# Two stacked cross attentions: a block's values in one stretch, its logits among the next block's queries

## The chip, the cores and the metric

The kernel runs on one core of one Trainium2 chip. The metric is the time of one execution on the device, in microseconds (us). The kernel before took 851.07 us in the median of three runs (849.96 to 851.61).

A core has engines that run their own instruction streams and meet only at semaphores: TensorE (PE, matmuls; PEld is its load of weights), VectorE (DVE), ScalarE (ACT), GpSimd (POOL) and SyncE (SP), which here issues nearly all DMAs. TensorE writes into PSUM, eight banks of 128 partitions by 512 floats; VectorE and ScalarE empty them; GpSimd works between tiles in SBUF only.

## The reference

Two cross attentions follow one another over 2 x 2048 query rows of width 512, both against the same context of 2 x 128 rows. All is float32. The change touches the first one:

```
q = x @ Wq0 + bq0            # 4096 x 1024, 16 heads of 64
k = ctx @ Wk0 + bk0 ; v = ctx @ Wv0 + bv0      # 128 keys for each of 2 batches
attn = (q . k) * mask[None]              # mask 0/1, per batch, query and key
attn = exp(attn - max(attn)) * mask
attn = attn / (sum over keys + 1e-15)
x1   = layernorm((attn @ v) @ Wo0 + bo0 + x) * gamma + beta
```

The second attention has 16 heads of 32, no mask, a softmax and a layer norm of its own.

## The kernel before, in words

The 4096 query rows are eight blocks (NB) of 512 (QB). Products that need precision are split in three: an operand is held as a high part rounded to fp32r and a low part that is the rest, and `split_product` (L501 to L503) adds high x low, low x high and high x high into one bank.

The kernel has two passes. The first pass makes, for each block, the queries, the logits, the exponentials and the unnormalised values with their sums, and stores these in DRAM. The second pass loads them, divides, applies the output matrix and the layer norm, and runs the whole second attention. The global maximum is kept as a running maximum over the blocks, so a block's exponentials can't start before the last of its logits is masked.

The first pass of one block i, by engine:

- TensorE. `queries0(i)` makes eight chunks of 128 query columns, each of twelve matmuls, alternately into bank 1 and bank 0 (`A_BANKS`). `logits0(i, c)` makes the logits of two heads, transposed (keys on partitions, 512 queries along), three matmuls a head, into four banks in turn (`L0_BANKS`: 0, 2, 3, 4). `values0(i, j)` makes value chunks 2j and 2j+1, each four matmuls of 32 columns (L557) into bank 5 or 6 (`U_BANKS`), and then the row sums of four heads (L540) into bank 7.
- ScalarE. `x_high` (L873) rounds a block's x, `mask_float` (L881) converts the integer mask `mask_raw` to `mask_f`, `q_high` (L885) takes a query chunk out of its bank, `exponential` (L891) does four heads in place in `scores`, `save_u` (L914, L918) copies value chunks and sums out of their banks.
- VectorE. `q_low` (L1148) makes the low part of a query chunk and frees its bank. `mask_scores` (L1159) takes one head's logits out of its bank times the mask, with their maximum. `running_max` (L1165 to L1182) reduces these to one number and ends with `neg_mx`. `mask_probs` (L1189) multiplies four heads of exponentials by the mask.
- GpSimd. `x_low` (L1548) makes the low part of x for the next block, `x_and_bias` (L1556) adds a bias to the natural rows of x.
- SP. One queue of DMA issues in program order, with its waits: for i = 1 to 7 the loads of x and the mask ahead, sums of block i - 2, the stores of block i - 1's values and sums, the store and next load of the natural rows.

Every engine runs its list in order, and the lists are written out by hand. Those of the middle of the first pass are, before the change:

```
PE :  for i in 1..7:  for j in 0..3: values0(i-1, j); logits0(i, 2j); logits0(i, 2j+1)
                      queries0(i+1)
ACT:  mask_float(i); x_high(i+1); save_u(i-1); then q_high(i+1, 0..7), exponential(i, 0..3) behind 1..4
DVE:  mask_scores(i) 16 heads; running_max(i); q_low(i+1, 0..7), mask_probs(i, 0..3) behind 2..5
```

The waits that the prediction goes through are these. A value chunk c waits for its four heads to be masked (`probs_ready`) and for the save that frees its bank (`u_saved`, two chunks back). Logits of heads 2c and 2c+1 wait for the masked scores that free the bank (`masked_ready`, four heads back) and for all of the block's q_low. A query chunk waits for the q_low two chunks back; chunk 1 also waits for masked scores, since bank 0 is shared with the logits. `mask_float(i)` overwrites the mask that `mask_probs(i-1)` reads, so it waits for `probs_ready`. Behind the last block TensorE makes the second attention's keys (L489, four products into banks 1, 0, 3, 4), then `values0(7, 0..3)`, then `output_first` (L632 to L636), the first product of the second pass.

Of the kernel before, what the change touches and what calls it, by code (L numbers as in the profile page):

```python
# [28 lines left out]
def cross_attention_program(nc, x_t, x_n, mask_t, ctx_t, wq0, wk0, wv0, wo0, wq1, wk1, wv1, wo1,  # L29
# [10 lines left out]
    with ExitStack() as ctx:  # L40
# [108 lines left out]


# [6 lines left out]
        A_BANKS, L0_BANKS = [bank[1], bank[0]], [bank[0], *bank[2:5]]  # L157
        U_BANKS, SUM_BANK = bank[5:7], bank[7]

        V0_BANKS = [*U_BANKS, SUM_BANK, U_BANKS[0]]  # L160
# [98 lines left out]
        def l0_bank(i, h):  # L259

            return L0_BANKS[(h + (i == 0)) % 4]
# [221 lines left out]
        def _(pe):  # L483
# [21 lines left out]
            def queries0(i):  # L505
                pe.wait_ge(x_ready, i + 1)
                if i == 0:
                    pe.wait_ge(x_half_ready, 1)
                    pe.wait_ge(kv_done, 2)
                for c in range(C0):  # L510
# [4 lines left out]
                    if c == 1 and i > 0:  # L515

                        pe.wait_ge(masked_ready, H0 * i - (HC0 if i > 1 else 0))
                    for k in range(KC):
                        cols = slice(c * P, (c + 1) * P)
                        last = split_product(A_BANKS[c % 2][:], (wq0_hi[:, k, cols], wq0_lo[:, k, cols]),  # L520
                                             (x_hi[:, k, :], x_lo[:, k, :]), k == 0, k == KC - 1)
                    last.then_inc(q_psum_ready, 1)

            def logits0(i, c):
# [19 lines left out]
            def values0(i, j):  # L544
                b = i // NBB
                for c in range(2 * j, 2 * j + 2):
# [5 lines left out]
                    if not (i == 0 and c < 2):  # L552
                        pe.wait_ge(u_saved, (C0 + 1) * i + (c - 1 if c >= 2 else c - 2))

                    for part in range(G):
                        h, first = HC0 * c + part // 2, c * P + 32 * part
                        last = nc.tensor.matmul(U_BANKS[c % 2][32 * part:32 * part + 32, :],  # L557
# [59 lines left out]
            pe.wait_ge(q_ready, C0 * NB)  # L617
            for n in range(C1):
                if n == 1:
# [226 lines left out]
        def _(act):  # L846
# [28 lines left out]
            def mask_float(i):  # L875
# [3 lines left out]
                if i > 0:  # L879
# [894 lines left out]
```

## Time and profile before

| | |
|---|---|
| median of three runs | 851.07 us (849.96 to 851.61) |
| the profiled execution | 850.99 us, its span 849.2 us |
| granted TensorE clock, mean | 0.995 |
| TensorE, matmul busy | 829.6 us (98% of the span) |
| VectorE busy | 569.9 us (67%) |
| GpSimd busy | 448.8 us (53%) |
| ScalarE busy | 403.1 us (47%) |
| DMA, mean rate | 132 GB/s |

The span runs from the first to the last instruction of one execution; the rest of an execution's time lies around it. Busy time counts overlapping matmuls once, and a busy TensorE need not be at its peak. The first pass ends at about 359 us of the span. In a timeline, equal neighbours of one line are merged (x16 is sixteen instructions), a start is in microseconds from the start of the span, and a bracket says how long the engine was idle before the row and what ended that. The start of a matmul to the start of the next is what one costs; its own length is longer, since they overlap.

### The profile page before, as it was taken

The page shows a single profiled execution, that of the slowest core. Times are in us where ns is not written, and L with a number is a line of the kernel's source. Part 1 is how long each engine was busy: PE and PEld are TensorE (multiplying, and loading weights), DVE is VectorE, ACT ScalarE, POOL GpSimd, SP SyncE. Part 2 cuts the span into 40 slices and gives each one's busy share as a digit, 9 for nine tenths or more (in the row PEclk, how much of TensorE's full clock was granted, in tenths as well). Part 3 has the DMA queues.
Part 4 walks back from the last instruction along what each step waited for, and adds up shares of the span by engine and source line. Part 5 has one row for each costly group of instructions (what it writes and reads, how often), then busy time and mean ns, then how long its engine had stood idle before and what let it go on. Part 6 is the DMA issues. An engine that isn't in the chain of part 4 may idle for free.

```text
span 849.2 us, 12709 instructions
## 1 busy us (share of the span) xinstructions
PE 829.6 (98%) x4652; PEld 561.8 (66%) x4652; DVE 569.9 (67%) x1307; ACT 403.1 (47%) x535; POOL 448.8 (53%) x285
## 2 busy tenths in 40 slices
PE   9999999999999999898999999999999999999996
PEld 6777475665657484385667577677676775776744
DVE  3567766767667585876766766747657567667587
ACT  4416373645546454733543634444536436354262
POOL 2022403123040405235878789689687886894446
PEclk9999999999999999998999999999999999999999
DMA  9518525161625044887360531433424515311002
GB/s 309 204 46 297 191 101 214 50 223 54 251 64 200 29 186 177 226 314 191 96 170 26 167 107 51 149 99 98 151 75 112 162 37 163 100 50 51 1 26 74
DMA packets 50429, 112.37 MB, mean 132 GB/s; under 512 B 4544, under 2 KB 10944, under 8 KB 50368
## 3 DMA queue, kind: packets, MB, share of 16 engines
q1 hardware_dynamic: 49408, 111.23, 40.3%
q8 instruction: 37, 0.61, 0.3%
q10 hardware_dynamic: 960, 0.34, 0.2%
q14 instruction: 24, 0.20, 0.1%
HBM read 77.47 MB, written 34.08 MB: 131 GB/s over the span
## 4 chain that ended last, share of the span: by engine, by line
PE 68%; POOL 12%; DVE 8%; issue 5%; DMA 3%; ACT 3%; SPq 1%; DVEq 0%; POOLq 0%; ACTq 0%
PE bank L501 15%; PE bank L502 15%; PE bank L503 14%; PE bank L557 7%; PE bank L533 6%; POOL a_raw L1585 4%; POOL a_lo L1590 4%; PE bank L540 3%; POOL a_lo L1596 3%; PE bank L695 3%; DVE scores L1304 2%; DMA r_bc<-r_dram 2%; ACT a_hi L968 1%; DMA wk_sb<-wk 1%; PE bank L667 1%
## 5 line engine op out<-in xcount | busy, mean ns | idle before, releaser
L1548 POOL TENSOR_TENSOR x_lo<-x_raw,x_hi 128x2048 fp32r<-128x2048 f32 (+1 forms) x8 | 35.6, 4448 | 196.3 <-ACT x_hi L873 180.7
L501 PE MATMUL bank<-wo_lo,a_hi 128*128 128x512 f32 x320 | 127.7, 399 | 0.0
L502 PE MATMUL bank<-wo_hi,a_lo 128*128 128x512 f32 x320 | 124.8, 390 | 0.0
L503 PE MATMUL bank<-wo_hi,a_hi 128*128 128x512 f32 x320 | 124.7, 390 | 0.0
L1159 DVE CUSTOM_DVE_ANT_0 scores<-bank,mask_f 128x512 f32<-128x512 f32 x128 | 80.8, 687 | 51.9 <-PE bank L533 51.9
L1590 POOL TENSOR_TENSOR a_lo<-a_raw,a_hi 128x1024 fp32r<-128x1024 f32 x32 | 77.4, 2421 | 50.9 <-ACT a_hi L968 50.9
L501 PE MATMUL bank<-x_lo,wq_hi 128*128 128x512 f32 x256 | 101.1, 395 | 0.5 <-DVE q_lo L1148 0.5
L988 ACT ACTIVATE scores<-scores,sh 128x512 f32<-128x512 f32 x128 | 80.3, 710 | 41.0 <-DVE sh L1329 41.0
L502 PE MATMUL bank<-x_hi,wq_lo 128*128 128x512 f32 x256 | 99.7, 390 | 0.0
L503 PE MATMUL bank<-x_hi,wq_hi 128*128 128x512 f32 x256 | 99.7, 389 | 0.0
L885 ACT ACTIVATE q_hi<-bank,bq_sb 128x512 fp32r<-128x512 f32 x64 | 44.1, 690 | 100.9 <-PE bank L503 97.3
L1304 DVE TENSOR_SCALAR_CACHE_REDUCE scores<-bank 128x512 f32<-128x512 f32 x128 | 80.6, 686 | 15.2 <-PE bank L695 15.2
L1148 DVE SCALAR_TENSOR_TENSOR q_lo<-bank,bq_sb,q_hi 128x512 fp32r<-128x512 f32 x64 | 47.7, 746 | 42.3 <-ACT q_hi L885 42.2
L501 PEld LDWEIGHTS bank<-wo_lo,a_hi 128*128 128x128 f32 x320 | 60.1, 188 | 22.5 <-issue 11.0
L968 ACT ACTIVATE a_hi<-a_raw 128x1024 fp32r<-128x1024 f32 x32 | 33.9, 1060 | 85.4 <-POOL a_raw L1585 80.3
L1189 DVE TENSOR_TENSOR scores<-scores,mask_f 128x2048 f32<-128x2048 f32 x31 | 72.0, 2323 | 0.6 <-ACT scores L891 0.6
L1585 POOL TENSOR_TENSOR a_raw<-a_raw,r_bc 128x1024 f32<-128x1024 f32 x28 | 67.1, 2396 | 7.2 <-DMA r_bc<-r_dram 7.2
L503 PEld LDWEIGHTS bank<-wo_hi,a_hi 128*128 128x128 f32 x320 | 60.1, 188 | 12.9
L502 PEld LDWEIGHTS bank<-wo_hi,a_lo 128*128 128x128 f32 x320 | 60.1, 188 | 11.7
L557 PE MATMUL bank<-scores,v 128*32 128x512 f32 x512 | 61.8, 598 | 4.3 <-ACT u_out L914 2.7
L540 PE MATMUL bank<-scores,summer 128*32 128x512 f32 x512 | 65.6, 595 | 0.0
L914 ACT ACTIVATE u_out<-bank 128x512 f32<-128x512 f32 x64 | 37.3, 597 | 56.5 <-PE bank L557 55.5
(179 smaller groups left out, 1668.1 us busy)
## 6 DMA issues: line engine op xcount, KB each, us to landing
u_dram<-u_out SPq DMA_DIRECT2D x8, 2048.0 KB, 7.3
a_raw<-u_dram SPq DMA_DIRECT2D x32, 512.0 KB, 3.7
r_bc<-r_dram SPq DMA_DIRECT2D x56, 256.0 KB, 5.0
x_raw<-x_t SPq DMA_DIRECT2D x8, 1024.0 KB, 5.6
xn<-x_n SPq DMA_DIRECT2D x8, 1024.0 KB, 5.3
xb_dram<-xn SPq DMA_DIRECT2D x8, 1024.0 KB, 5.8
z<-xb_dram SPq DMA_DIRECT2D x32, 256.0 KB, 2.9
out<-z SPq DMA_DIRECT2D x6, 1024.0 KB, 7.3
```

The source lines that it names most:

```text
L501: nc.tensor.matmul(dst, lh, rl, start=first, stop=False)
L502: nc.tensor.matmul(dst, ll, rh, start=False, stop=False)
L503: return nc.tensor.matmul(dst, lh, rh, start=False, stop=last)
L533: last = nc.tensor.matmul(l0_bank(i, HC0 * c + a)[:], kk[r, c, ks], qq[r, c, :], start=(n == 0), stop=(n == 2))
L540: last = nc.tensor.matmul(dst[32 * g:32 * g + 32, :], summer[:, j, :], scores[:, G * j + g, :], start=(j == 0), stop=(j == HG - 1))
L557: last = nc.tensor.matmul(U_BANKS[c % 2][32 * part:32 * part + 32, :], v0[:, b, first:first + 32], scores[:, h, :], start=True, stop=True)
L988: nc.scalar.activation(scores[:, h, :], scores[:, h, :], ACT.Exp, bias=sh1[:, g, h:h + 1], scale=SCALE1).then_inc(probs1_ready, 1)
L1159: nc.vector.tensor_tensor_reduce(out=scores[:, h, :], in0=l0_bank(i, h)[:], in1=mask_f[:], scale=1.0, scalar=-3e38, op0=ALU.mult, op1=ALU.max,
L1189: nc.vector.tensor_tensor(four, four, mask_f[:].unsqueeze(1).to_broadcast([P, HG, QB]), ALU.mult).then_inc(probs_ready, 1)
L1304: nc.vector.tensor_scalar(scores[:, h, :], L_BANKS[h % HC1][:], 1.0, -3e38, ALU.mult, ALU.max, accum_out=mx1[:, h:h + 1]).then_inc(scores1 ...
L1585: nc.gpsimd.tensor_tensor(a_raw[:, n, :], a_raw[:, n, :], r_bc[:, n % 2, :], ALU.mult).then_inc(attn0_ready, 1)
L1590: nc.gpsimd.tensor_tensor(a_lo[:, n, :], a_raw[:, n, :], f(a_hi[:, n, :]), ALU.subtract).then_inc(a0_ready, 1)
```

## The change

The list of TensorE for blocks i = 1 to 6 is now: all four `values0(i-1, j)`; then four times two `logits0` of block i and one chunk of `queries0(i+1)`; then the other four chunks of queries. Block 7, which has no next block, keeps values and logits in turns. VectorE takes q_low of the next block's chunks 0 to 3 between each four heads of masked scores, the running maximum after that, and the four `mask_probs` behind q_low of chunks 5, 6, 7, the last two in a row. ScalarE does its four exponentials behind q_high of chunks 4 to 7; it saves two value chunks, then does x_high and the mask, then saves the others.

The values get four banks (3 to 6) in blocks 0 to 5, two (6 and 1) in block 6, four (5, 6, 2, 1) in block 7. The logits get banks 2 to 5 (block 0 as it was). Where a bank is shared a wait is added: logits 0 and 1 wait for saves 4 and 6 of the block before, value chunk 1 of block 6 for a q_low, chunk 3 of block 7 for a key product; the masked-score wait of the queries goes, but for block 1. The mask of the last block is converted in place, so its conversion doesn't wait for `mask_probs(6)`.

```diff
+        def mask_of(i):
+            return mask_f[:] if i < NB - 1 else mask_raw[:].bitcast(f32)
...
-        A_BANKS, L0_BANKS = [bank[1], bank[0]], [bank[0], *bank[2:5]]
-        U_BANKS, SUM_BANK = bank[5:7], bank[7]
+        A_BANKS, L0_BANKS = [bank[1], bank[0]], bank[2:6]
+        U_BANKS, U_AMONG, U_END, SUM_BANK = bank[3:7], [bank[6], bank[1]], [bank[5], bank[6], bank[2], bank[1]], bank[7]
+        def u_banks(i):
+            return U_BANKS if i < NB - 2 else (U_AMONG if i == NB - 2 else U_END)
...
-            def queries0(i):
+            def queries0(i, first=0, last=C0):
...
-                    if c == 1 and i > 0:
-                        pe.wait_ge(masked_ready, H0 * i - (HC0 if i > 1 else 0))
+                    if c == 1 and i == 1:
+                        pe.wait_ge(masked_ready, H0)
...
@@ logits0 @@
+                if 0 < i < NB - 1 and c < 2:
+                    pe.wait_ge(u_saved, (C0 + 1) * (i - 1) + (5 if c == 0 else 7))
...
@@ values0 @@
-                    if not (i == 0 and c < 2):
-                        pe.wait_ge(u_saved, (C0 + 1) * i + (c - 1 if c >= 2 else c - 2))
+                    n = len(u_banks(i))
+                    if c >= n:
+                        pe.wait_ge(u_saved, (C0 + 1) * i + c - n + 1)
+                    elif i >= NB - 2:
+                        pe.wait_ge(u_saved, (C0 + 1) * i)
+                        if i == NB - 2 and c == 1:
+                            pe.wait_ge(q_ready, C0 * NB - 1)
+                        if i == NB - 1 and c == 3:
+                            pe.wait_ge(kv1_done, 1)
...
@@ TensorE's list @@
-            for i in range(1, NB):
+            for i in range(1, NB - 1):
                 for j in range(HG):
                     values0(i - 1, j)
-                    for c in range(2 * j, 2 * j + 2):
-                        logits0(i, c)
-                if i + 1 < NB:
-                    queries0(i + 1)
+                for c in range(HG):
+                    logits0(i, 2 * c)
+                    logits0(i, 2 * c + 1)
+                    queries0(i + 1, c, c + 1)
+                queries0(i + 1, HG, C0)
+            for j in range(HG):
+                values0(NB - 2, j)
+                for c in range(2 * j, 2 * j + 2):
+                    logits0(NB - 1, c)
             pe.wait_ge(kv1_loaded, 32)
             pe.wait_ge(q_ready, C0 * NB)
+            pe.wait_ge(u_saved, (C0 + 1) * (NB - 2) + C0)
             for n in range(C1):
-                if n == 1:
+                if n == 2:
                     pe.wait_ge(masked_ready, H0 * NB)
...
@@ output0 @@
+                    elif i == 0:
+                        pe.wait_ge(u_saved, (C0 + 1) * NB)
...
@@ mask_float @@
-                if i > 0:
+                if 0 < i < NB - 1:
                     act.wait_ge(probs_ready, HG * i)
-                nc.scalar.activation(mask_f[:], mask_raw[:], ACT.Copy).then_inc(mask_ready, 1)
+                nc.scalar.activation(mask_of(i), mask_raw[:], ACT.Copy).then_inc(mask_ready, 1)
...
@@ ScalarE's list; block 0's exponentials stay behind q_high(1, 1..4) @@
-                if i > 0:
-                    mask_float(i)
-                    x_high(i + 1)
-                    save_u(i - 1)
+            for i in range(1, NB - 1):
+                save_u(i - 1, 0, 2)
+                x_high(i + 1)
+                mask_float(i)
+                save_u(i - 1, 2)
                 for c in range(C0):
                     q_high(i + 1, c)
-                    if 1 <= c <= HG:
-                        exponential(i, c - 1)
+                    if c >= HG:
+                        exponential(i, c - HG)
+            save_u(NB - 2, 0, 2)
             mask_float(NB - 1)
-            save_u(NB - 2, 0, 6)
+            save_u(NB - 2, 2, 6)
...
@@ VectorE's list; block 0 as it was @@
-            for i in range(NB - 1):
-                mask_scores(i)
+            for i in range(1, NB - 1):
+                for c in range(HG):
+                    mask_scores(i, HG * c, HG * (c + 1))
+                    q_low(i + 1, c)
                 running_max(i)
-                for c in range(1, C0):
+                q_low(i + 1, HG)
+                for c in range(HG + 1, C0):
                     q_low(i + 1, c)
-                    if 2 <= c < HG + 2:
-                        mask_probs(i, c - 2)
+                    mask_probs(i, c - HG - 1)
+                mask_probs(i, HG - 1)
```

## Rows read from the trace of the kernel before

**Rows 1.** Waits of TensorE, 0 to 420 us: waiting line, released by; total us, times, longest.

```profile
PE bank L557 <- ACT u_out L914: 2.7, 3, 1.6
PE bank L695 <- DVE q_lo L1297: 2.7, 1, 2.7
```

**Rows 2.** TensorE's timeline, values of block 2, logits of block 3: start, length us.

```profile
162.59 1.92 PE L557 MATMUL bank<-scores,v 128*32 128x512 f32 x16
164.33 1.04 PE L540 MATMUL bank<-scores,summer 128*32 128x512 f32 x8
165.31 0.50 PE L533 MATMUL bank<-q_lo,k_hi 64*128 64x512 f32 x2
...
166.89 1.92 PE L557 MATMUL bank<-scores,v 128*32 128x512 f32 x16
```

**Rows 3.** TensorE's timeline, first queries of block 4, values of block 3.

```profile
179.78 0.50 PE L501 MATMUL bank<-x_lo,wq_hi 128*128 128x512 f32 x1
180.12 0.40 PE L502 MATMUL bank<-x_hi,wq_lo 128*128 128x512 f32 x1
...
201.77 1.92 PE L557 MATMUL bank<-scores,v 128*32 128x512 f32 x16
```

**Rows 4.** Timeline of TensorE, last values and the first output product.

```profile
353.62 1.92 PE L557 MATMUL bank<-scores,v 128*32 128x512 f32 x16 [0.63 <-ACT u_out L914]
...
356.19 1.93 PE L557 MATMUL bank<-scores,v 128*32 128x512 f32 x16
...
358.91 0.50 PE L632 MATMUL bank<-wo_lo,a_hi 128*128 128x512 f32 x1
```

**Rows 5.** Timeline of TensorE, queries followed by logits, block 0.

```profile
42.13 0.39 PE L503 MATMUL bank<-x_hi,wq_hi 128*128 128x512 f32 x1
42.45 0.49 PE L533 MATMUL bank<-q_lo,k_hi 64*128 64x512 f32 x2
```

**Rows 6.** Timeline of ScalarE: exponential of block 2; behind block 3's queries.

```profile
149.69 2.00 ACT L891 ACTIVATE scores<-scores,neg_mx 128x2048 f32<-128x2048 f32 x1
...
162.70 0.69 ACT L885 ACTIVATE q_hi<-bank,bq_sb 128x512 fp32r<-128x512 f32 x1 [2.03 <-PE bank L503]
163.29 0.62 ACT L881 ACTIVATE mask_f<-mask_raw 128x512 f32<-128x512 int32 x1
163.81 1.90 ACT L873 ACTIVATE x_hi<-x_raw 128x2048 fp32r<-128x2048 f32 x1
```

**Rows 7.** Timeline of VectorE, running maximum and masked probabilities of block 2.

```profile
142.69 0.17 DVE L1165 TENSOR_REDUCE tile_mx<-maxes 128x1 f32<-128x16 f32 x1
...
144.88 0.15 DVE L1182 TENSOR_SCALAR neg_mx<-m_all 128x1 f32<-128x1 f32 x1
...
150.49 2.28 DVE L1189 TENSOR_TENSOR scores<-scores,mask_f 128x2048 f32<-128x2048 f32 x1
152.69 0.74 DVE L1148 SCALAR_TENSOR_TENSOR q_lo<-bank,bq_sb,q_hi 128x512 fp32r<-128x512 f32 x1
```

**Rows 8.** The page's groups, value saves: count, busy us, mean ns, idle before.

```profile
L914 ACT ACTIVATE u_out<-bank 128x512 f32<-128x512 f32 x64 | 37.3, 597 | 56.5 <-PE bank L557 55.5
```

**Rows 9.** Timeline of TensorE, values of block 0, second group.

```profile
88.53 1.92 PE L557 MATMUL bank<-scores,v 128*32 128x512 f32 x16 [0.48 <-ACT u_out L914]
```

**Rows 10.** The page's groups, masked scores.

```profile
L1159 DVE CUSTOM_DVE_ANT_0 scores<-bank,mask_f 128x512 f32<-128x512 f32 x128 | 80.8, 687 | 51.9 <-PE bank L533 51.9
```

**Rows 11.** Timeline of VectorE, masked probabilities of block 7.

```profile
347.45 2.29 DVE L1189 TENSOR_TENSOR scores<-scores,mask_f 128x2048 f32<-128x2048 f32 x1 [0.44 <-ACT scores L891]
...
352.48 2.29 DVE L1189 TENSOR_TENSOR scores<-scores,mask_f 128x2048 f32<-128x2048 f32 x1 [0.20 <-ACT scores L891]
```

**Rows 12.** Timelines of GpSimd and VectorE where they overlap, block 0.

```profile
67.48 4.63 POOL L1556 TENSOR_TENSOR xn<-xn,bo_b 128x2048 f32<-128x2048 f32 x1
...
70.65 3.61 DVE L1189 TENSOR_TENSOR scores<-scores,mask_f 128x2048 f32<-128x2048 f32 x1
```

**Rows 13.** Windows, TensorE alone: busy us, matmuls, granted clock, DMA share, GB/s.

```profile
400.00:402.00 2.00, 2.00 (x5) 0.50 1.00 227
```

More of the change, by code:

```diff
@@ L259, in l0_bank @@
         def l0_bank(i, h):
-            return L0_BANKS[(h + (i == 0)) % 4]
+            return A_BANKS[1] if i == 0 and h % 4 == 3 else L0_BANKS[h % 4]
         def heads(c):
@@ L503, in split_product @@
                 return nc.tensor.matmul(dst, lh, rh, start=False, stop=last)
-            def queries0(i):
[L506 to L510, printed above, removed]
+            def queries0(i, first=0, last=C0):
+                if first == 0:
+                    pe.wait_ge(x_ready, i + 1)
+                    if i == 0:
+                        pe.wait_ge(x_half_ready, 1)
+                        pe.wait_ge(kv_done, 2)
+                for c in range(first, last):
                     if i == 0 and c % 2 == 0:
@@ L913, in save_u @@
                     act.wait_ge(u_psum_ready, C0 * i + c + 1)
-                    nc.scalar.activation(u_out[:, :, c, :], U_BANKS[c % 2][:].rearrange("p (t q) -> p t q", t=QT),
+                    nc.scalar.activation(u_out[:, :, c, :], u_bank(i, c)[:].rearrange("p (t q) -> p t q", t=QT),
                                          ACT.Copy).then_inc(u_saved, 1)
@@ L944, in _ @@
             x_high(1)
-            for i in range(NB - 1):
-                if i > 0:
-                    mask_float(i)
-                    x_high(i + 1)
-                    save_u(i - 1)
+            for c in range(C0):
+                q_high(1, c)
+                if 1 <= c <= HG:
+                    exponential(0, c - 1)
+            for i in range(1, NB - 1):
[3 more added lines that the diff above has]
+                save_u(i - 1, 2)
                 for c in range(C0):
                     q_high(i + 1, c)
-                    if 1 <= c <= HG:
-                        exponential(i, c - 1)
+                    if c >= HG:
+                        exponential(i, c - HG)
+            save_u(NB - 2, 0, 2)
             mask_float(NB - 1)
-            save_u(NB - 2, 0, 6)
+            save_u(NB - 2, 2, 6)
             wo0_high(0)
@@ L1150, in q_low, with mask_scores @@
                                                op0=ALU.add, op1=ALU.subtract).then_inc(q_ready, 1)
-            def mask_scores(i):
-                dve.wait_ge(mask_ready, i + 1)
-                for h in range(H0):
+            def mask_scores(i, first=0, last=H0):
+                if first == 0:
+                    dve.wait_ge(mask_ready, i + 1)
+                for h in range(first, last):
                     if i == 0 and h in V0_AFTER:
@@ L1158, in mask_scores @@
                     nc.vector.nop(nofuse=True)
-                    nc.vector.tensor_tensor_reduce(out=scores[:, h, :], in0=l0_bank(i, h)[:], in1=mask_f[:],
+                    nc.vector.tensor_tensor_reduce(out=scores[:, h, :], in0=l0_bank(i, h)[:], in1=mask_of(i),
                                                    scale=1.0, scalar=-3e38, op0=ALU.mult, op1=ALU.max,
@@ L1188, in mask_probs @@
                 four = scores[:, HG * j:HG * (j + 1), :]
-                nc.vector.tensor_tensor(four, four, mask_f[:].unsqueeze(1).to_broadcast([P, HG, QB]),
+                nc.vector.tensor_tensor(four, four, mask_of(i).unsqueeze(1).to_broadcast([P, HG, QB]),
                                         ALU.mult).then_inc(probs_ready, 1)
@@ L1211, in _ @@
                     wv0_low(c)
-            for i in range(NB - 1):
-                mask_scores(i)
+            mask_scores(0)
+            running_max(0)
+            for c in range(C0):
+                q_low(1, c)
+                if 2 <= c < HG + 2:
+                    mask_probs(0, c - 2)
+            for c in range(C1):
+                query_bias(c)
+            for i in range(1, NB - 1):
+                for c in range(HG):
+                    mask_scores(i, HG * c, HG * (c + 1))
+                    q_low(i + 1, c)
                 running_max(i)
-                for c in range(1, C0):
+                q_low(i + 1, HG)
+                for c in range(HG + 1, C0):
                     q_low(i + 1, c)
-                    if 2 <= c < HG + 2:
-                        mask_probs(i, c - 2)
-                if i == 0:
-                    for c in range(C1):
-                        query_bias(c)
+                    mask_probs(i, c - HG - 1)
+                mask_probs(i, HG - 1)
             mask_scores(NB - 1)
```

14 lines of the change are left out of this document (7 added, 7 removed).

## The prediction, as it was put on record

> **What bounds the kernel now.** I read three views. The waits of TensorE over the first 420 us come first: all that it waited for bank saves in the first pass is 2.7 us, in three places [rows 1]. The other wait shown there, 2.7 us for a q_lo, lies in the second pass. So the first pass is bound by TensorE's instruction stream, and a new order can win only by making the stream itself shorter or by removing those few waits. The timeline of TensorE is next. In a middle block the stretch from one value group to the next is 162.59 to 166.89, 4.30 us: values 1.74, row sums 0.97, logits 1.58 [rows 2]. Queries from first chunk to next values take 179.78 to 201.77, 21.99 us [rows 3]. A block is 4 x 4.30 + 21.99 = 39.19 us. Last come the timelines of VectorE and ScalarE, because the change makes their finish times matter.
>
> **The stream of a middle block.** The same instructions run, in another order, so the count of matmuls drops out and only the changes of kind are left. A value group that follows another one costs 356.19 - 353.62 = 2.57 us [rows 4], against 1.74 + 0.97 = 2.71 where logits follow and precede. Three of the four groups get the short form: 3 x 2.57 + 2.71 = 10.42, a gain of 0.42. The logits keep their 1.58, which already holds an entry and an exit. The queries are cut into five pieces where there was one: four pieces lie behind logits, and three times more than before they are entered and left. A first query matmul takes 0.34 (179.78 to 180.12) against a plain step of some 0.23, so 0.11 for an entry [rows 3]; a last one before logits 0.32 (42.13 to 42.45), so 0.09 for an exit [rows 5]. 3 x 0.20 = 0.60 lost. Together +0.18 by these rounded rows, +0.12 when I add up the whole block with unrounded steps; I take **+0.15 us a block, +0.9 for the six blocks** (1 to 6) that get the new order. Bounds: 0 (the two changes of kind cost the same) and 1.5.
>
> **The new race at the seventh value chunk.** Masking the probabilities (L1189), which stood early in a block's queries, now ends after the next values have begun, and the float mask (L881) waits for it on ScalarE with the saves of chunks 2 to 7 queued behind it. With four banks, value chunk 6 wants the bank of chunk 2. Both sides start at the end of the fourth, last interleaved query chunk; call it 0.
> - TensorE: four chunks more of 12 x 0.2265 = 2.72 us and an exit, values start at 10.96; chunk 6 is due 0.02 + 3 x 2.57 = 7.73 later, at 18.69.
> - VectorE and ScalarE: q_hi starts 0.19 after the last matmul and takes 0.69 [rows 6]; q_lo may go on at 0.91 and occupies 0.67; the running maximum, 144.88 - 142.69 = 2.19 [rows 7], gives neg_mx at 3.77; the first exponential starts at 3.96 and holds ScalarE 1.89 of its 2.00 [rows 6]; q_hi, q_lo bring 7.24; then four mask steps at 2.20 (150.49 to 152.69 [rows 7]) with two q_lo of 0.66 among them: the fourth starts at 15.16 and ends at 17.44, that is 6.48 after the values began. Signal 0.08, mask conversion 0.52 (163.29 to 163.81 [rows 6]), save 0.60 [rows 8] and 0.13 for its signal: 18.77.
>
> So chunk 6 waits 0.08 us; both sides hang on the same event, so it doesn't add up over blocks. With five such blocks (1 to 5 of the values): **+0.4**. The bounds are 0 and, if each mask step holds VectorE for nearly its full 2.3 us and ACT's steps are also whole, 0.6 a block, 3.0. The other new deadlines hold on the same clock: mask steps 2 and 3 end at 12.4 and 15.2, values want them at 13.6 and 16.1; query chunk 6 wants q_lo of chunk 4 at 5.4 and has it at 4.6; logits 0 and 1 want saves 4 and 6, done 1 us and more ahead; POOL's x_lo (4.6 us) ends 11.1 after the values start, the next queries begin at 12.1. SP's queue still has the whole block: its u store moves about 1 us earlier, its x load 2.5 us later and 22 us ahead of use. None costs.
>
> **Block 1.** The wait of 0.48 at 88.53 for the save of chunk 0 [rows 9] goes, since four banks serve. What is late next is chunk 6: values start at 88.53 - 0.48 - 4.30 - 0.06 = 83.7, so it is due at 91.4; the saves start at 87.8, and two saves (0.96), x_hi (1.80 [rows 6]), the mask (0.52) and the save of chunk 2 with its signal (0.73) free it at 91.8. 0.4 for 0.5: **-0.1**, bounds -0.5 and +0.5.
>
> **Block 7, the last logits.** Here the old order stays, values group by group with logits between, but VectorE comes to it late: the fourth mask step of block 6 frees it only 6.40 us after the values start, where before it was idle and took the first logits at 3.8. The four logits banks are full by then. The fifth and sixth head (due 4.30 + 2.71 = 7.01) need two heads masked: 6.40 + 0.61 + 0.74 = 7.75 (0.63 us a head [rows 10], its signal after 0.74). The next pair needs four: 6.40 + 3 x 0.61 + 0.74 = 8.97, due at 7.75 + 0.80 = 8.55. 0.74 + 0.42 and a restart of 0.1: **+1.3**. VectorE then catches up (2.45 a group against 4.30). The mask converted in place only keeps ScalarE out of this; had it waited, the saves behind it would have come later too. Bounds 0.5 and 2.1, from the start of the heads 0.4 earlier or 0.4 later for each of the two waits.
>
> **The last values.** Before, they wait for two-bank saves, the third time until 353.62 (0.63), and end at 358.91 [rows 1, 4]. With four banks they follow the masks: chunk 2 at 347.45 + 2.29 = 349.74, then 2.57 to 352.4 (the third mask ended before 352.48), 2.57 more to 354.9, where the fourth mask (352.48 + 2.29 = 354.77 [rows 11]) is just done; then 2.72 to 357.6. **-1.3**. The DMA issues and a_hi that follow hang on the same end and move with it. Bounds: -1.6 and 0, the latter if the first a_hi or a_lo takes over (the first a_lo is wanted 3.8 us later and is there with 1 us left; the second is about 0.2 late, but the next long wait, for q_lo, hangs on DMAs that moved the whole 1.3).
>
> **Sum.** 0.9 + 0.4 - 0.1 + 1.3 - 1.3 = +1.2 us. The profiled execution took 850.99 with a span of 849.2, the median of three is 851.07, 0.1 apart; so 852.2 beside either.
>
> **One thing that speaks against the change.** VectorE and POOL get in each other's way: a mask step that began at 70.65 while POOL's add of 67.48 to 72.11 ran took 3.61 in place of 2.28, so it did next to nothing until POOL was done [rows 12]. In the new order x_lo and the fourth mask step meet. The mask step starts 4.2 us after the values begin, x_lo at the earliest at 5.4 (two saves, x_hi), so it is POOL that waits, and has time. The Trainium skill, SBUF — State Buffer, section Who interferes with whom, says that a VectorE instruction with two SBUF inputs contends with POOL's reads, and that issue order decides who blocks. By that rule the margin of 1.2 us is all there is; the trace agrees in its one row (1.33 us lost), and the case in which the order turns is a rival below.
>
> **Rivals.**
> 1. Faster: the clock. TensorE's clock is granted at half (1.2 of 2.4 GHz) from about 398 to 404.6, behind the 2.7 us wait for q_lo [rows 1, 13], where a query step takes 0.43 in place of 0.23; some 12 steps and the logits before them lose 2.7 us. The tail's -1.3 shortens the wait by about 0.2 at most and everything comes 1 us later, so it may be judged otherwise: 852.2 - 2.7 = 849.5, and with a stream cost of 0 and the block 1 gain whole, 848.4. It is faster from the point where the clock doesn't fall. For: one wait alone causes it. Against: that wait stays almost as it is. Chance 0.15.
> 2. The values' gain counts and the extra query pieces don't: a piece behind logits starts without the 0.20. Then -0.4 a block, 852.2 - 0.9 - 2.5 = 848.8. Against: each of the other changes of kind shows its price. Chance 0.07.
> 3. The seventh chunk waits for real (0.6 a block): 852.2 + 2.6 = 854.8. For: the margin is -0.08, and the chain has some twenty steps. Chance 0.20.
> 4. The tail's gain doesn't come, since another engine's finish takes over: 853.5. Chance 0.10.
> 5. x_lo gets in ahead of the fourth mask step: it ends 5.4 + 4.6 + 2.3 = 12.3 after the values start in place of 6.5, each block waits about 5.8, 29 in all: 881. Chance 0.03.
>
> My forecast gets 0.45. Below 0.2% (1.7 us) a measurement of this kernel can't be told from no change: 849.4 to 852.8 is the same. The forecast lies near the upper edge; of its 0.45 I give 0.32 to the same and 0.13 to slower; rivals 3 to 5 add 0.29 to slower (of 4 a little falls below); rivals 1 and 2 share out as 0.16 faster, 0.06 the same. With 0.04 of the slow side moved to the same for what cancels: faster 0.16, same 0.42, slower 0.42. The range takes in rivals 1 to 4: 848.6 to 855.4.
>
> **What would show it.** A middle block of some 39.3 to 39.5 us between its values; value groups 2.57 apart; query pieces that start with 0.34 and end with 0.32; a wait of TensorE at the values (L557 before, the same line after) for u_out of at most 0.2 a block; the float mask starting right at the end of the fourth mask step; two waits of 1.2 together for masked scores in the last logits; the last values without a wait for saves, ending 1.3 sooner from the last logits. I am wrong in substance if a block comes out under 39.1, if the seventh chunk waits over 0.4, or if the fourth mask step takes over 2.5 us.

## The result, and the profile after

The changed kernel took 854.58 us in the median of five runs (853.44 to 856.28), the kernel before 851.07 (849.86 to 851.61) beside it: a ratio of 1.0040, 95% interval 1.0023 to 1.0056. It is about 3.4 us slower, where 1.2 was forecast. The profiled execution took 853.44 us (span 851.6). Two later sets gave 1.0041 (1.0025 to 1.0056) and 1.0050 (1.0031 to 1.0068).

Three points of the trace cut the profiled executions up: V0, the first value matmul of block 0; V7, the first of block 7; O, the first output product. In microseconds, from the timelines of TensorE:

| stretch | before | after | difference | forecast |
|---|---|---|---|---|
| values of block 0 to values of block 1 | 39.72 | 39.87 | +0.15 | +0.05 |
| five middle blocks (values 1 to values 6) | 195.89 | 197.82 | +1.93 | +1.15 |
| values 6 to V7 | 26.30 | 27.69 | +1.39 | +1.3 |
| V7 to O | 13.31 | 12.06 | -1.25 | -1.3 |
| V0 to O | 275.22 | 277.44 | +2.22 | +1.2 |
| O to the end of the span | 490.3 | 490.5 | +0.2 | 0 |

The waits of TensorE from 0 to 420 us after the change (waiting line, what released it; total us, times, longest), which answer to [rows 1] (dots stand for rows left out here and below):

```profile
PE bank L730 <- DVE q_lo L1344: 2.7, 1, 2.7
PE bank L582 <- DVE scores L1235: 2.0, 1, 2.0
...
PE bank L582 <- DVE scores L1228: 1.1, 1, 1.1
PE bank L549 <- DVE maxes L1200: 1.0, 2, 0.8
...
PE bank L582 <- ACT u_out L949: 0.2, 1, 0.2
```

The 2.7 us for saves are gone but for 0.2; in their place stand 1.0 for masked scores and 1.1 for a mask step, which no longer hides behind a save. The 2.0 is the wait for the mask of V7 itself; before, it was 1.6. A middle block on TensorE, the values of block 1 with what follows (start, length us), beside [rows 2, 3]:

```profile
123.56 1.92 PE L582 MATMUL bank<-scores,v 128*32 128x512 f32 x16
...
126.16 1.90 PE L582 MATMUL bank<-scores,v 128*32 128x512 f32 x16
...
128.74 1.90 PE L582 MATMUL bank<-scores,v 128*32 128x512 f32 x16
...
131.39 1.92 PE L582 MATMUL bank<-scores,v 128*32 128x512 f32 x16
...
134.10 0.50 PE L549 MATMUL bank<-q_lo,k_hi 64*128 64x512 f32 x2
...
135.36 0.40 PE L549 MATMUL bank<-q_hi,k_hi 64*128 64x512 f32 x2
135.69 0.50 PE L513 MATMUL bank<-x_lo,wq_hi 128*128 128x512 f32 x1
136.03 0.39 PE L514 MATMUL bank<-x_hi,wq_lo 128*128 128x512 f32 x1
...
138.32 0.39 PE L515 MATMUL bank<-x_hi,wq_hi 128*128 128x512 f32 x1
138.64 0.50 PE L549 MATMUL bank<-q_lo,k_hi 64*128 64x512 f32 x2
...
163.11 1.92 PE L582 MATMUL bank<-scores,v 128*32 128x512 f32 x16
```

Value groups follow 2.60 and 2.58 apart; the fourth is 131.39 - 128.74 = 2.65, so chunk 6 waited about 0.08. Then 134.10 to 163.11, 29.01 us, are logits and queries. The block is 163.11 - 123.56 = 39.55. What its seventh value chunk hung on, in the timelines of VectorE, GpSimd and ScalarE:

```profile
125.55 4.48 DVE L1228 TENSOR_TENSOR scores<-scores,mask_f 128x2048 f32<-128x2048 f32 x2
...
129.10 5.37 POOL L1595 TENSOR_TENSOR x_lo<-x_raw,x_hi 128x2048 fp32r<-128x2048 f32 x1 [29.12 <-ACT x_hi L908]
...
130.13 0.63 ACT L916 ACTIVATE mask_f<-mask_raw 128x512 f32<-128x512 int32 x1 [1.10 <-DVE scores L1228]
130.66 2.53 ACT L949 ACTIVATE u_out<-bank 128x512 f32<-128x512 f32 x5
```

The third and fourth mask step end at 130.03 (125.55 + 4.48), 6.47 behind the start of the values (forecast 6.48); the mask conversion starts at 6.57, right behind. POOL's x_lo, which began 1.35 after the fourth mask step did, took 5.37, where the same x_lo took 4.59 before the change: it gave way, as forecast, for some 0.8. Block 1's wait for the save, beside [rows 9], and the two waits among the last logits with what VectorE did before them:

```profile
88.86 1.90 PE L582 MATMUL bank<-scores,v 128*32 128x512 f32 x16
...
91.83 1.92 PE L582 MATMUL bank<-scores,v 128*32 128x512 f32 x16 [0.20 <-ACT u_out L949]
...
329.22 0.51 PE L549 MATMUL bank<-q_lo,k_hi 64*128 64x512 f32 x2 [0.76 <-DVE maxes L1200]
...
330.44 0.50 PE L549 MATMUL bank<-q_lo,k_hi 64*128 64x512 f32 x2 [0.25 <-DVE maxes L1200]
...
323.37 4.48 DVE L1228 TENSOR_TENSOR scores<-scores,mask_f 128x2048 f32<-128x2048 f32 x2
327.77 0.68 DVE L1200 CUSTOM_DVE_ANT_0 scores<-bank,mask_raw 128x512 f32<-128x512 f32 x1
```

Last, the values of block 7, beside [rows 4]: the only wait left is for the mask step, none for a save.

```profile
353.27 1.92 PE L582 MATMUL bank<-scores,v 128*32 128x512 f32 x16 [1.14 <-DVE scores L1228]
...
355.87 1.90 PE L582 MATMUL bank<-scores,v 128*32 128x512 f32 x16
...
358.44 1.90 PE L582 MATMUL bank<-scores,v 128*32 128x512 f32 x16
...
361.13 0.50 PE L664 MATMUL bank<-wo_lo,a_hi 128*128 128x512 f32 x1
```

### The profile page after: what moved, and what is told of

Read it like the earlier page. It is cut to its first block, busy times and chain, and to the rows that moved or that the text cites. A ratio compares the mean times of both kernels' runs of the same rounds, so it can differ in the third digit from the quotient of the medians.

```text
span 851.6 us, 12688 instructions
## 1 busy us (share of the span) xinstructions
PE 831.9 (98%) x4652; PEld 562.3 (66%) x4652; DVE 571.5 (67%) x1307; ACT 399.0 (47%) x535; POOL 453.8 (53%) x285
## 4 chain that ended last, share of the span: by engine, by line
PE 70%; POOL 12%; DVE 9%; issue 4%; ACT 2%; DMA 2%; SPq 0%; DVEq 0%; POOLq 0%; ACTq 0%
PE bank L513 16%; PE bank L514 14%; PE bank L515 14%; PE bank L582 6%; PE bank L549 6%; POOL a_raw L1632 4%; POOL a_lo L1637 4%; PE bank L556 3%; POOL a_lo L1643 3%; PE bank L730 3%; DVE scores L1351 2%; PE bank L501 2%; DMA r_bc<-r_dram 2%; ACT a_hi L1008 1%; PE bank L702 1%
## 5 line engine op out<-in xcount | busy, mean ns | idle before, releaser
L1595 POOL TENSOR_TENSOR x_lo<-x_raw,x_hi 128x2048 fp32r<-128x2048 f32 (+1 forms) x8 | 39.4, 4929 | 197.2 <-ACT x_hi L908 197.2
L513 PE MATMUL bank<-x_lo,wq_hi 128*128 128x512 f32 x256 | 103.3, 403 | 0.5 <-DVE q_lo L1188 0.5
L1200 DVE CUSTOM_DVE_ANT_0 scores<-bank,mask_f 128x512 f32<-128x512 f32 x112 | 70.6, 685 | 34.7 <-PE bank L549 34.7
L1228 DVE TENSOR_TENSOR scores<-scores,mask_f 128x2048 f32<-128x2048 f32 x28 | 64.8, 2331 | 0.0
L926 ACT ACTIVATE scores<-scores,neg_mx 128x2048 f32<-128x2048 f32 x31 | 62.0, 2000 | 2.1 <-DVE neg_mx L1223 2.1
```

What stands on the lines that cost most here:

```text
L513: nc.tensor.matmul(dst, lh, rl, start=first, stop=False)
L926: nc.scalar.activation(four, four, ACT.Exp, bias=neg_mx[:]).then_inc(exp_ready, 1)
L1200: nc.vector.tensor_tensor_reduce(out=scores[:, h, :], in0=l0_bank(i, h)[:], in1=mask_of(i), scale=1.0, scalar=-3e38, op0=ALU.mult, op1=ALU ...
L1228: nc.vector.tensor_tensor(four, four, mask_of(i).unsqueeze(1).to_broadcast([P, HG, QB]), ALU.mult).then_inc(probs_ready, 1)
```

## The experiments

Ratios are to the kernel before, run beside each on the same chip, with their 95% intervals; a ratio of 1.001 is 0.85 us. "Of one run" means a single time. What is left open by the result is why the first pass grew by 2.2 and not 1.2, and why executions grew by 3.4 when the first pass grew by 2.2.

**The last values' part alone.** The kernel before, with four banks for block 7 (and the waits that these banks need, left out here):

```diff
+        U_END = [bank[5], bank[6], bank[2], bank[1]]
+        def u_banks(i):
+            return U_BANKS if i < NB - 1 else U_END
```

> The old order in every block; only the values of the last block get four banks (5, 6, 2, 1) in place of two. Theory A (terms add up one by one: the last values waited for bank saves): the stretch from the first values of block 7 to the first output product shrinks from 13.3 us to 12.1 us, as it did in the changed kernel (349.07 to some 361.1), every block before it stays at 39.18, and the time falls by 1.2 to 849.8. Rival R (the gain is given back in the second pass, where GpSimd's products with loaded data set the pace): the stretch shrinks, but the time stays at 851.1.

Measured: blocks of 39.18 as before, V7 to O 12.06 instead of 13.31. The 1.25 is there in full at the first output product, from the banks alone. The ratio is 0.9991 (0.9981 to 1.0002), -0.8 us; its interval (-1.6 to +0.2) holds both the whole 1.25 and nothing.

**The order alone, with its late mask work mended.** The changed kernel with the fourth mask step of block 6 behind four heads of masked scores, and four saves ahead of x_high:

```diff
-                mask_probs(i, HG - 1)
-            mask_scores(NB - 1)
+                if i < NB - 2:
+                    mask_probs(i, HG - 1)
+            mask_scores(NB - 1, 0, HG)
+            mask_probs(NB - 2, HG - 1)
+            mask_scores(NB - 1, HG)
...
-                save_u(i - 1, 0, 2)
+                save_u(i - 1, 0, 4)
                 x_high(i + 1)
                 mask_float(i)
-                save_u(i - 1, 2)
+                save_u(i - 1, 4)
```

> The new order with its two waits taken away: four value chunks are saved before x_hi and the mask (was two), and the fourth mask step of block 6 comes behind the first four masked heads of block 7. Theory A: no wait for saves at value chunk 6, no wait for masked scores in the last logits; a middle block 39.49 us (39.57 in the changed kernel, 39.18 before), the last logits 1.4 us shorter, the first pass ends 0.3 us later than before: 851.4. Theory H (about 1.3 us of the changed kernel's +3.5 lie in how often the TensorE clock is at half in the second pass, by the new order's own doing): 852.7. Rival B (what a block lost are not changes of kind but such waits): a middle block at 39.2 and 849.5.

Measured: the fourth value group starts without a wait, 2.57 behind the third in place of 2.65, and the block falls from 39.56 to 39.46; values 6 to V7 fall from 27.69 to 26.45. One new wait comes, once, in block 1, since x_high, and with it x_lo, starts two saves later. TensorE's timeline:

```profile
96.25 0.50 PE L513 MATMUL bank<-x_lo,wq_hi 128*128 128x512 f32 x1 [0.66 <-POOL x_lo L1598]
...
131.46 1.90 PE L582 MATMUL bank<-scores,v 128*32 128x512 f32 x16
```

V0 to O is 276.01, 1.43 less than the changed kernel's; the ratio is 1.0027 (1.0017 to 1.0037). With no wait left in a middle block it still takes 0.28 more than before (39.46 against 39.18): that is the price of the order itself, and I had put it at 0.15.

**More changes of kind.** Each of the four interleaved query chunks cut in two, one half behind each pair of heads (`queries0` is given the range of its steps):

```diff
                     logits0(i, 2 * c)
+                    queries0(i + 1, c, c + 1, range(0, 2))
                     logits0(i, 2 * c + 1)
-                    queries0(i + 1, c, c + 1)
+                    queries0(i + 1, c, c + 1, range(2, KC))
```

> The new order, but each interleaved query chunk is cut in two halves of six matmuls, one behind each two heads of logits: four query pieces and four logits pieces more in each of blocks 1 to 6, the same matmuls. Theory A (a change of kind costs TensorE some 0.1 us on either side): 4 x (0.11 + 0.09 + 0.11 + 0.10) = 1.6 us more a block, 41.2 in place of 39.57, and the execution 9.8 us longer than the changed kernel's 853.4 to 854.6: 863 to 864.5. Rival B (changes of kind cost nothing in this setting, the block's loss has another cause): 39.6 a block and 854.

Measured: a block is 41.26, 1.70 more, so 0.42 for one more change from logits to queries and back; 865.89 us in its one run. In its timeline:

```profile
137.75 0.39 PE L550 MATMUL bank<-q_hi,k_hi 64*128 64x512 f32 x2
138.07 0.50 PE L513 MATMUL bank<-x_lo,wq_hi 128*128 128x512 f32 x1
138.41 0.39 PE L514 MATMUL bank<-x_hi,wq_lo 128*128 128x512 f32 x1
...
139.34 0.40 PE L515 MATMUL bank<-x_hi,wq_hi 128*128 128x512 f32 x1
139.66 0.50 PE L550 MATMUL bank<-q_lo,k_hi 64*128 64x512 f32 x2
140.00 0.39 PE L550 MATMUL bank<-q_hi,k_lo 64*128 64x512 f32 x2
```

A change shows on both sides of it: the step before costs 0.32 (137.75 to 138.07) and the one behind it 0.34 (138.07 to 138.41), against a plain 0.23; and again 0.32 and 0.34 on the way back.

**The new order with two banks at the end** (its two bank waits moved to value chunk 1).

```diff
-            return U_BANKS if i < NB - 2 else (U_AMONG if i == NB - 2 else U_END)
+            return U_BANKS if i < NB - 2 else U_AMONG
```

> The changed kernel with two banks (6 and 1) for the last block's values in place of four. Theory A: from the first values of block 7 to the first output product 13.3 us in place of 12.1, the first pass ends 3.4 us later than before the change, time 854.7 to 855.8 (1.2 over the changed kernel's). Rival R (the second pass absorbs it): the stretch grows, the time stays at 853.4 to 854.6.

Measured: the waits for saves are back, V7 to O is 13.29, V0 to O 278.50. Its timeline:

```profile
353.25 1.92 PE L582 MATMUL bank<-scores,v 128*32 128x512 f32 x16 [1.12 <-ACT u_out L949]
...
356.66 1.92 PE L582 MATMUL bank<-scores,v 128*32 128x512 f32 x16 [0.63 <-ACT u_out L949]
```

But its one run took 852.73, under all of the changed kernel's. More runs of it follow below.

**The change again.**

> The changed kernel itself, unaltered, beside the same runs of the kernel before as the three others here. Its first pass was 2.2 us longer in the profiled execution, its median 3.5 us longer over five runs. Theory A (the first pass is all that the change does; what lies behind it varies by DMA landings and by how many stretches at half clock an execution has): +2.2, 853.4. Theory H (the new order also costs about 1.3 us in the second pass each time): +3.5, 854.8.

Measured: 1.0041 (1.0025 to 1.0056), the same as the first time. V0 to O is 277.35, but O to the end is 492.9, where the first profile had 490.5: the second pass differs by 2.4 between two executions of one kernel.

**The fourth mask step later, alone** (the first part of the mended version's diff).

> The changed kernel with one edit: VectorE takes the fourth mask step of block 6 behind the first four masked heads of block 7 in place of ahead of them. Theory A (the last logits wait because VectorE comes late to them): from the values of block 6 to those of block 7 26.3 us in place of 27.7, no wait of TensorE for masked scores; a middle block stays at 39.57 and the values of block 1 to 6 at 197.8. Rival (the wait is for the four logits banks themselves, not for when VectorE starts): 27.7 as before.

Measured: no wait for masked scores in block 7, values 6 to V7 26.44 in place of 27.69; blocks stay at 39.56; 854.25 in its one run. So 1.25 of block 7's 1.39 is VectorE's late arrival.

**x_lo ahead of the fourth mask step**, the rival at 881:

```diff
-                x_high(i + 1)
+                if i == 1:
+                    x_high(i + 1)
...
                     q_high(i + 1, c)
+                    if c == C0 - 1 and i < NB - 2:
+                        x_high(i + 2)
```

> The changed kernel, but ScalarE makes x_hi ahead of the block's last exponential, so that GpSimd's x_lo is ready to start while VectorE still has its third and fourth mask step to do. Theory A (a VectorE product of two SBUF tiles and a GpSimd one exclude each other, and the one that is ready first goes first): x_lo starts when the third mask step ends, the fourth waits 4.6 us for it, ends some 11 us after the values start, and value chunk 6 waits 4 to 5 us a block: 44 us a block in place of 39.57, the execution 20 to 25 us longer. Rival (both run side by side at a small cost): x_lo runs beside the mask steps, 39.6 to 40.5 a block.

Measured: 887.28 in its one run; a middle block takes 45.5 to 45.6, and 46.6 in two of the five. Its timelines of VectorE, GpSimd and TensorE, then TensorE's window (busy us, matmuls, granted clock, DMA share, GB/s):

```profile
174.23 6.30 DVE L1231 TENSOR_TENSOR scores<-scores,mask_f 128x2048 f32<-128x2048 f32 x1 [0.25 <-ACT scores L926]
...
172.38 6.01 POOL L1598 TENSOR_TENSOR x_lo<-x_raw,x_hi 128x2048 fp32r<-128x2048 f32 x1 [32.98 <-ACT x_hi L908]
...
181.88 3.56 PE L582 MATMUL bank<-scores,v 128*32 128x512 f32 x16 [4.25 <-ACT u_out L949]
...
183.00:185.00 2.00, 2.00 (x12) 0.50 0.30 105
```

The mask step took 6.30 in place of 2.28 and ended at 180.53, 2.1 after POOL (178.39), so it did its work behind POOL's. (POOL's own step is longer than its 4.6 because it began at 172.38 while VectorE's third mask step, 171.69 to 173.97, still ran.) TensorE waited 4.25 in each block, and on restart its clock was granted at half (1.2 GHz) for a while: the value group's row is 3.56 long where it is 1.92 at the full clock. A wait of 4.25 where there was 0.08 leaves 1.8 of the 6.0 a block to the clock. The prediction's rival had 5.8 a block, all of it waiting: the wait was over-counted and the clock left out.

**Weights' high parts sooner, on top of the last values' part.** ScalarE makes the two high parts of the output weights two saves sooner each, so that POOL's low parts don't meet VectorE's maximum:

```diff
-            save_u(NB - 2, 0, 6)
+            save_u(NB - 2, 0, 4)
             wo0_high(0)
-            save_u(NB - 2, 6)
+            save_u(NB - 2, 4, 6)
             wo0_high(1)
+            save_u(NB - 2, 6)
```

> The old order with four banks for the last values, and ScalarE rounds the two halves of the output weights two saves earlier each, so that GpSimd has done its second wo_lo before the last running maximum. In the kernel before, the small product L1179 of that maximum took 2.6 us in place of 0.7, until GpSimd's wo_lo had ended. Theory A (these terms add): L1179 takes 0.7, from the values of block 6 to those of block 7 24.4 to 24.5 us in place of 26.3, to the first output product 12.3, and the execution 3.2 us shorter than before: 848.0 by a before of 851.2. Rival R (the chain of DMAs at the start of the second pass doesn't move as much): the first pass ends 3 us sooner, the execution is 1 to 2 us shorter.

Measured: the running maximum's product (m_all) took 0.69 in place of 2.56; V0 to V7 is 1.62 less than before, V0 to O 3.11 less. Yet the ratio is 0.9991 (0.9981 to 1.0000), the same -0.8 us as without this step. Its waits up to 420 us show where some of it can go:

```profile
PE bank L710 <- DVE q_lo L1313: 3.8, 1, 3.8
PE bank L509 <- DVE z L1295: 1.6, 1, 1.6
...
PE bank L509 <- POOL a_lo L1606: 0.7, 1, 0.7
PE bank L682 <- ACT z L988: 0.7, 1, 0.7
```

All four lie behind O and make 6.8 us; the kernel before has 2.7 there [rows 1]. In this execution TensorE comes sooner and waits for work on the other engines that has not moved with it. It is one execution, and the slowest of the twelve (852.76, median 850.70), so 6.8 is more than such an execution will wait as a rule.

**Two banks at the end, timed in full.**

> The changed kernel with two banks for the last block's values, as in the run of that name before, now timed in full. Its profile had the first output product 1.06 us later after the first values than the changed kernel (278.50 against 277.44), yet its single time was below the changed kernel's. Theory S (the second pass absorbs what the tail gains, since its first wait for q_lo hangs on transfers that don't all move with it): the same execution as the changed kernel, 1.0041 of the kernel before, within 0.0007; rest of the span after the first output product 1.0 to 1.5 us shorter than the changed kernel's. Rival T (the tail's gain passes whole into the execution, my prediction's step): 1.2 us more than the changed kernel, 1.0055. Rival U (four banks at the end cost more behind the first output product than they win ahead of it): 852.7, 1.0014.

Measured: 1.0039 (1.0021 to 1.0056), with V0 to O at 278.69. Two banks in place of four cost 1.25 at O and nothing that can be seen in the execution (its interval still reaches the 1.2). The 852.7 of the single run was scatter, and the rival built on it (852.7, a ratio of 1.0014) falls.

**The change a third time, beside it.**

> The changed kernel once more, unaltered, beside the two-bank version on the same chip, so that the two are compared directly. All theories: 3.5 us above the kernel before (ratio 1.0041, 1.003 to 1.005), middle block 39.55, 277.4 from first values to first output product. Theory S: rest of the span 490.5 to 493, above the kernel before's by 1.3 in the mean; rival T: the rest as in the kernel before, 490.3, and the 492.9 of the repeat was a stray.

Measured: 1.0050 (1.0031 to 1.0068); V0 to O 277.50; O to the end 490.2. Where the kernel before ran at half clock [rows 13], this execution did not; its one half-clock stretch ahead of the span's last 4 us lies at 349.7 to 353.1, in the values of block 7 behind TensorE's wait of 1.95. Two windows of TensorE, as in [rows 13]:

```profile
402.00:404.00 2.00, 1.85 (x16) 1.00 0.96 215
404.00:406.00 2.00, 2.00 (x11) 1.00 1.10 250
```

**The kernel before again, for a second profile.**

> The kernel before, unaltered, for a second profile: how much the rest of the span after the first output product differs between executions of one kernel. Theory S: 490.3 again within 0.5, since its tail leaves nothing to absorb. Rival T (it is scatter of the clock): it differs by 1 us or more, as the changed kernel's two profiles do (490.5 and 492.9). Both: 39.18 a block, 275.2 from first values to first output product.

Measured: 39.18 a block and 275.21 from V0 to O, as the first time; O to the end 492.2, against 490.3. So "490.3 again within 0.5" was wrong: what lies behind O differs by 2 us between executions of one kernel, the one before or the changed one.

**Where the executions part.** The traces say more when they are cut twice behind O: at Q, where TensorE restarts behind its wait for q_lo (403.02 in the second profile of the change), and at A, the first product behind its last wait for GpSimd's a_lo (448.44 there). In us:

| profile | V0 to O | O to Q | Q to A | A to the end |
|---|---|---|---|---|
| before | 275.22 | 39.26 | 46.70 | 404.3 |
| before again | 275.21 | 39.40 | 47.09 | 405.7 |
| the change | 277.44 | 39.57 | 46.90 | 404.0 |
| again | 277.35 | 41.90 | 45.42 | 405.6 |
| a third time | 277.50 | 40.77 | 45.21 | 404.3 |
| mended | 276.01 | 40.98 | 45.16 | 405.6 |
| before, four banks at the end | 273.97 | 39.92 | 45.21 | 405.6 |
| the same, weights' high parts sooner | 272.11 | 43.98 | 45.71 | 405.7 |

Behind A every version takes 404.0 to 404.3 or 405.5 to 405.7, and nothing between (the three profiles of such versions that the table leaves out too). The longer ones, and they alone, have a half-clock stretch of 3.4 us at about 820 us, so that stretch costs 1.4 when it comes there. TensorE's windows, second and third profile of the change:

```profile
820.00:822.00 2.00, 2.00 (x7) 0.60 0.00 0
...
820.00:822.00 2.00, 2.00 (x13) 1.00 0.01 4
```

So no version changes anything behind A, and the last 404 us of the span can be left out of the account. From V0 to A the kernel before took 361.2 and 361.7, the changed one 363.9, 364.7 and 363.5: 2.6 more in the mean.

## Why the prediction was right or wrong

The kernel came out slower by more than the forecast, near the third rival's 854.8, but not by that rival's mechanism: it had the seventh value chunk wait 0.6 a block, and the chunk waited the forecast 0.08. What failed is the size of the stream term and, less surely, the step from the first pass to the execution.

- **What bounds it.** Right: TensorE's own stream, and the first pass changed by what changed on that stream.
- **The stream of a middle block, +0.15.** The direction was right, the size half of what was measured. The mended version has 0.28 a block with no wait in it. The failed step is "3 x 0.20 = 0.60 lost" against "a gain of 0.42". From rows of the changed kernel, logits and queries take 29.01, before 4 x 1.58 + 21.99 = 28.31: 0.70 lost. The values, 134.10 - 123.56 less the 0.08 of waiting, take 10.46 against 4 x 2.71 = 10.84: 0.38 gained. Net 0.32, and the 39.46 of the mended version gives 0.28. Both orders have nine changes of kind a block; three pairs of logits and values became three of logits and queries (the queries lie in four pieces, not in the five that the prediction names; its sum rightly has three more). The prices of the single steps were near: 0.20 on the queries' side and 1.58 less six plain steps of 0.23, so 0.20, on the logits', make 0.40 a pair, and 0.42 was measured. But the term is a small difference between two larger ones, and an error of some hundredths in each doubled it. Six blocks: +1.7 in place of +0.9.
- **The seventh value chunk, 0.08 a block.** Right, and shown: with four saves first the fourth group follows 2.57 behind the third in place of 2.65, and the block falls by 0.10. The rival at 0.6 a block falls.
- **Block 1, -0.1.** Right. The fourth group stands 2.97 behind the third (88.86 to 91.83), 0.39 more than the second and third groups of block 1, of which the profile calls 0.20 a wait; before, the second group stood 4.84 behind V0 in place of 4.30 [rows 9]. A gain of 0.15 against the stream's 0.28: the stretch grew by 0.15.
- **Block 7, +1.3.** Right: waits of 0.76 and 0.25, +1.39 in all, gone but for 0.14 when VectorE is given the first four heads ahead of the mask step.
- **The last values, -1.3.** Right up to the first output product (-1.25), shown by both bank experiments. Open behind it is "The DMA issues and a_hi that follow hang on the same end and move with it", the step by which the sum passes the whole gain on to the execution. The four banks alone brought 0.8 of the 1.25 in the median, and their profile has 85.1 from O to A, against 86.0 and 86.5 before, so it shows nothing given back. Where more was won (3.11 at O, with the weights' high parts sooner) the execution still gained only 0.8 (0.0 to 1.6): there the step fails.

How much of each part reaches the execution shows when the versions stand side by side. Differences to before in us; the last column is the ratio's, times 851:

| version | V0 to V7 | V0 to O | execution |
|---|---|---|---|
| the change | +3.47 | +2.22 | +3.4 (2.0 to 4.8) |
| again | +3.31 | +2.13 | +3.5 (2.1 to 4.8) |
| a third time | +3.45 | +2.28 | +4.3 (2.6 to 5.8) |
| two banks at the end | +3.47 | +3.47 | +3.3 (1.8 to 4.8) |
| mended | +2.04 | +0.79 | +2.3 (1.4 to 3.1) |
| before, four banks at the end | 0.00 | -1.25 | -0.8 (-1.6 to +0.2) |
| the same, weights' high parts sooner | -1.62 | -3.11 | -0.8 (-1.6 to 0.0) |

The first pass gives the change +2.2; its three medians lie at +3.4 to +4.3. Two readings of the surplus are left.

The first: the execution goes with the start of the last block's values (V0 to V7), within 0.9 in every row, while it is off from the first output product by 1.2 to 2.3 in five of the seven. What is won between V7 and O would then be given back behind O, as rival 4 had it but a step later, and the change would cost 1.9 + 0.15 + 1.4 = 3.5. For it speaks the last row. Against it speak two profiles: that of the four banks alone, and the mended version's, in which TensorE's wait for q_lo swallows a gain made ahead of V7 (4.07, against 2.71 to 3.21 in the change's three; Q comes 317.0 behind V0 there and in the change's first profile).

The second: the executions pass on V0 to O and differ besides in the granted clock. Over all timed executions its mean was 0.9947 after the change (18 runs) and 0.9963 before (56), and 0.9932 in the mended version (11 runs) against 0.9965 in the runs beside it (23). Among those of before, a clock lower by 0.001 goes with 0.37 us, which would make 0.6 of the change's surplus of 1.2 and 1.2 of the mended version's 1.5; in the last row it would explain 0.4 of 2.3. So neither reading fits every row, and the intervals are 1.6 to 3.2 us wide: the cause of the 1.2 behind O stays open. So does whether the order of the work lowers the clock.

**Rival 1, the clock.** The half-clock stretch behind the q_lo wait did shorten: 3.4 us in place of 6.8 in the first profile after, of which two windows stand here, and none in the third.

```profile
400.00:402.00 2.00, 1.30 (x14) 1.00 0.86 311
...
402.00:404.00 2.00, 2.00 (x7) 0.56 1.05 250
```

The time didn't fall: without it O to the end was 490.2, with the full 6.8 it was 490.3. From Q to A, where the stretch lies, the third profile is 1.5 and 1.9 shorter than the two of before (45.21 against 46.70 and 47.09), so that much of the forecast 2.7 was there; O to Q was longer by 1.4 to 1.5, and took it back. **Rival 2** (query pieces that cost nothing) falls by the 0.42 a pair. **Rival 5**: the margin of 1.2 us held, and the price is real, +32 us in one run where it is lost.

Both orders of the two engines are now seen: mask step first, x_lo 5.37 long; x_lo first, the mask step 6.30 long in place of 2.28. By the Trainium skill, SBUF — State Buffer, section Who interferes with whom, issue order decides who blocks; these two rows agree.

No version beat the kernel before by more than its measurement is uncertain.

## What to carry to other kernels

When TensorE is full, count the changes of kind pair by pair, and take a pair's price from a whole stretch of the timeline, not from the one slow step; here a pair cost 0.42 us between logits and queries and 0.35 between logits and values (4.30 less 2.57 less six plain steps of 0.23), so trading three for three was already a loss of 0.21 of the 0.28. Before a gain at a hand-over between stages is counted, add up the waits behind it: where the stage already waits for another engine, the gain can be lost there, as most of 3.11 us was with the weights' high parts sooner. When single profiles of one kernel differ by 2 us, cut them at waits that all versions share and see which stretches stay the same: here 404 of 850 us did, but for one half-clock stretch. And an order that puts another engine's work late should be followed to the last turn of the loop, where the next consumer comes sooner than in the middle.

## What the runs showed of the hardware

- A change of kind on TensorE costs on both sides: 0.32 for the last step before and 0.34 for the first behind, against 0.23.
- The clock after a wait is not the same from run to run. Behind a wait of 2.65 to 3.2 us for q_lo the rows show it at half at once (both profiles before), from some 1.5 us after the restart (first profile after), some 0.9 us after it (second), or not at all up to 412 us (third profile after).
- A half-clock stretch of 3.4 us at about 820 us came in some executions of each kernel and not in others; it cost 1.4 us (405.6 in place of 404.2 from A to the end).
- A VectorE step on two SBUF operands that starts during a GpSimd step of the same kind doesn't share: 6.30 in place of 2.28. A GpSimd step that starts during VectorE's took 5.37 and 6.01 in place of 4.6.
